# One chunk of a shared expert moved from before to behind a block loop, and a router's ranking placed ahead of a weight split

## What is computed

```
x = layernorm(x + attention(x))                        # 4096 tokens of 256
probs = softmax(x @ gate_w.T); idx = top_k(probs + gate_b, 6)
for each expert e of 16:                               # H = 176
    y += c[:, e] * ((silu(x @ W1.T + B1) * (x @ W3.T + B3)) @ W2.T + B2)
z = (silu(x @ ws1.T + bs1) * (x @ ws3.T + bs3)) @ ws2.T + bs2     # 352 wide, every token
out = layernorm(x + y + z)
```

## Time and profile before

| | |
|---|---|
| three runs, median | 1126.18 us (1124.87 to 1127.89) |
| the profiled execution | 1117.81 us, of which the span is 1115.7 |
| PE busy | 1033.5 us, 93% of the span |
| POOL, DVE, ACT busy | 738.6, 759.2, 674.3 us |
| attention, router and tiles in front | up to about 563 us |
| the loop over blocks | about 565 to 1055 us |
| behind the loop | 1055 to 1115.7 us |

### The profile page before, as it was taken

How to read it: one execution, slowest core, us unless ns; L and a number is a source line. 1 busy time by engine, 2 the same in 40 slices (tenths; PEclk the granted TensorE clock), 3 DMA queues, 4 the chain that set the end, 5 groups by cost and what they waited for, 6 DMA issues and landing times.

```text
span 1115.7 us, 28318 instructions
## 1 busy us (share of the span) xinstructions
PE 1033.5 (93%) x8028; PEld 845.6 (76%) x8029; DVE 759.2 (68%) x2406; ACT 674.3 (60%) x1680; POOL 738.6 (66%) x671
## 2 busy tenths in 40 slices
PE   7899998989999997798988999999999999999993
PEld 4546564646555553478988999999999999999993
DVE  8786878786878787668756555555555555555467
ACT  3567676767676765755545555555555555555546
POOL 4223368887888888866725666666666666666667
PEclk9999999999999999989999999999999999999997
DMA  6624254545454635466957666777776777777686
GB/s 186 184 75 115 77 141 149 166 143 159 139 172 134 180 128 163 147 214 218 293 162 165 110 117 121 117 117 118 118 120 113 119 119 117 118 117 121 114 238 237
DMA packets 127036, 163.53 MB, mean 147 GB/s; under 512 B 18800, under 2 KB 107504, under 8 KB 126704
## 3 DMA queue, kind: packets, MB, share of 16 engines
q1 hardware_dynamic: 82240, 99.73, 31.0%
q0 software_dynamic: 39024, 54.29, 27.6%
q10 hardware_dynamic: 5696, 8.55, 2.5%
HBM read 65.36 MB, written 73.85 MB: 125 GB/s over the span
## 4 chain that ended last, share of the span: by engine, by line
PE 74%; DVE 12%; ACT 4%; issue 4%; DMA 3%; POOL 2%; SPq 1%; ACTq 0%; POOLq 0%; DVEq 0%
PE psum L1061 18%; PE psum L1088 13%; PE psum L796 10%; PE psum L838 5%; PE psum L826 5%; PE psum L811 4%; PE psum L1046 4%; PE psum L1072 4%; PE psum L1057 3%; DVE rowmax L1501 3%; ACT probs L1164 2%; PE psum L1027 2%; PE psum L813 2%; PE psum L870 1%; DMA stack_q<-shift_l 1%
## 5 line engine op out<-in xcount | busy, mean ns | idle before, releaser
L1164 ACT ACTIVATE probs<-psum 128x512 f32<-128x512 f32 (+2 forms) x384 | 186.4, 529 | 115.8 <-PE psum L826 113.6
L1501 DVE TENSOR_REDUCE rowmax<-psum 128x1 f32<-128x512 f32 (+3 forms) x352 | 212.5, 633 | 60.5 <-PE psum L813 58.1
L2030 POOL DMA_INDIRECT xs_d<-x1p,index x192 | 204.5, 1065 | 52.5 <-issue 45.3
L2098 POOL DMA_INDIRECT x_d<-y_sb,tokens x104 | 162.9, 1566 | 98.6 <-ACT y_sb L1358 48.6
L2098 POOL DMA_INDIRECT z_d<-y_sb,tokens x103 | 161.2, 1565 | 81.4 <-issue 39.4
L1840 DVE TENSOR_TENSOR xb_lo<-psum,xb_hi 128x256 fp32r<-128x256 f32 x207 | 87.9, 425 | 186.2 <-ACT xb_hi L1155 186.2
L1061 PE MATMUL psum<-we_hi_lo,xb_hi 128*128 x828 | 200.6, 323 | 0.0
L1088 PE MATMUL psum<-we_hi_lo,hb_hi 88*128 (+1 forms) x828 | 174.6, 304 | 0.0
L1358 ACT ACTIVATE y_sb<-psum,combine 128x256 f32<-128x256 f32 x207 | 98.4, 475 | 125.0 <-PE psum L1088 112.4
L811 PE MATMUL psum<-stack_k,stack_q 96*128 96x256 bf16 (+3 forms) x512 | 139.0, 311 | 10.9 <-DVE rowmax L1501 4.8
L1061 PEld LDWEIGHTS psum<-we_hi_lo,xb_hi 128*128 128x128 f32 x828 | 146.6, 189 | 0.1
(11 more groups left out here) (206 smaller groups left out, 2326.4 us busy)
## 6 DMA issues: line engine op xcount, KB each, us to landing
xb<-xs_d SPq DMA_DIRECT2D x207, 138.0 KB
stack_q<-q_h SPq DMA_DIRECT2D x48, 128.0 KB
stack_k<-k_h SPq DMA_DIRECT2D x45, 128.0 KB
w_raw<-in_we SPq DMA_DIRECT2D x9, 608.0 KB, 4.4
xT_raw<-in_xT SPq DMA_DIRECT2D x9, 512.0 KB
stack_q<-q_m SPq DMA_DIRECT2D x32, 128.0 KB
stack_k<-k_m SPq DMA_DIRECT2D x32, 128.0 KB
x_res<-in_x SPq DMA_DIRECT2D x8, 512.0 KB, 3.7
```

Source lines behind the costliest of these rows:

```text
L1164: nc.scalar.activation(probs[kt][:, heads[0]:heads[0] + n, :], st[f % ST_BANKS][:, 0:n * width].rearrange("p (h t) -> p h t", h=n), ACT.Ex ...
L1501: nc.vector.reduce_max(rowmax[gpar][:, heads[0]:heads[0] + n, qt], src, AX.X).then_inc(sm_free, 1)
L2030: nc.gpsimd.indirect_dma_start(out=xs_d[:, :], out_offset=bass.IndirectOffsetOnAxis(ap=index[tp][:, n:n + 1], axis=0), in_=x1p[tp][:, n // ...
L2098: nc.gpsimd.indirect_dma_start(out=(x1_d, z_d)[k % 2][:, :], out_offset=bass.IndirectOffsetOnAxis(ap=tokens[:, k:k + 1], axis=0), in_=y_sb ...
```

## The change

1. `HC1` goes from 10 to 9: nine chunks (27 tiles) stand in front of the loop and seven (21 tiles) behind. The tile numbers of the epilogue, weights, scatters and pads stay.
2. A third turn of the block loop is written out, and three of the five late x1 chunks are loaded there (at blocks 20, 22, 23) instead of in the last turn. The other two are loaded behind the first two z loads of the finals.
3. Each late chunk is split into halves of its own (`x1T_tail`), and earlier: at T1 + 2, 3, 4, 8, 9. The hidden products behind the loop get buffers of their own.
4. The finals' statistics begin behind tile T1 + 6 instead of T1 + 8, and POOL makes 4 sums ahead instead of 3.
5. In DVE's stream, from tile 9 on, `split_w` stands behind the epilogue's stage instead of ahead of it.

```diff
-HC1 = 10
+HC1 = 9
-LATE_TURNS = 2
+LATE_TURNS = 3
-FINAL_FROM, SUMS_AHEAD = T1 + 8, 3
+FINAL_FROM, SUMS_AHEAD = T1 + 6, 4
+X1T_LATE_AT = {20: 0, 22: 1, 23: 2}
+X1T_SPLIT_AT = {2: 0, 3: 1, 4: 2, 8: 3, 9: 4}
+W_ITEM_BEHIND_STAGE = 9
...
+        def x1_halves(hc):
+
+            return X1T[hc % 2] if hc <= HC1 + 1 else X1T_tail[hc - HC1 - 2]
+
+        def hidden_of(T):
+
+            return [bufs[bank_of(T)] for bufs in (front_h if T < T1 else tail_h)]
...
         def split_x1_of(T):
 
+            if T >= T1 + 2:
+                hc = HC1 + 2 + X1T_SPLIT_AT.get(T - T1, HALVES)
+                return hc if hc < HALVES else None
...
-                    if last and k < len(x1T_late):
-                        load_x1T(HC1 + 2 + k)
+                    if isinstance(j0, int) and j0 + k in X1T_LATE_AT:
+                        sp.wait_ge(late_w_lo, 2 * LATE_W)
+                        load_x1T(HC1 + 2 + X1T_LATE_AT[j0 + k])
...
                 for i in FINAL_ORDER[:FINAL_FIRST]:
                     load_final(i, src, dst)
+                if n == 1:
+                    for hc in range(HC1 + 2 + len(X1T_LATE_AT), HALVES):
+                        load_x1T(hc)
...
-                if T in W_ITEM_AT:
+                if T in W_ITEM_AT and T < W_ITEM_BEHIND_STAGE:
                     split_w(W_ITEM_AT[T])
                 if T >= 5 and (T - 5) % ST == 0 and T < T1 - 1:
                     shared_out((T - 5) // ST)
                 epilogue(T)
+                if T in W_ITEM_AT and T >= W_ITEM_BEHIND_STAGE:
+                    split_w(W_ITEM_AT[T])
```

More of the change, by code:

```diff
@@ L244, in postln_layer @@
     phase_a = ExitStack()
-    phase_b, phase_w, phase_z, phase_l = ExitStack(), ExitStack(), ExitStack(), ExitStack()
+    phase_b, phase_w, phase_z, phase_l, phase_x = [ExitStack() for _ in range(5)]
     def sem(name):
@@ L368, in postln_layer @@
         phase_l.close()
-        hidden = [sb(f"hidden{n}", [P, HT_TOK]) for n in range(2)]
-        h_hi = [sb(f"h_hi{n}", [P, HT_TOK], f32r) for n in range(2)]
-        h_lo = [sb(f"h_lo{n}", [P, HT_TOK], f32r) for n in range(2)]
+        x1T_late = [sb(f"x1T_late{n}", [P, KD, HT_TOK], where=phase_x) for n in range(len(X1T_LATE_AT))]
+        phase_x.close()
+        front_h = [[sb(f"{name}{n}", [P, HT_TOK], dt) for n in range(2)]
+                   for name, dt in (("hidden", fp32), ("h_hi", f32r), ("h_lo", f32r))]
         X1T = [sb(f"x1T_{n}", [P, 2, KD, HT_TOK], f32r) for n in range(2)]
@@ L382, in postln_layer @@
         phase_b.close()
-        x1T_late = [sb(f"x1T_late{n}", [P, KD, HT_TOK]) for n in range(HALVES - HC1 - 2)]
+        tail_h = [[sb(f"tail_{name}{n}", [P, HT_TOK], dt) for n in range(2)]
+                  for name, dt in (("hidden", fp32), ("h_hi", f32r), ("h_lo", f32r))]
+        x1T_late += [sb(f"x1T_late{n}", [P, KD, HT_TOK]) for n in range(len(X1T_LATE_AT), HALVES - HC1 - 2)]
         fin_x = [sb(f"fin_x{n}", [P, HALF, D]) for n in range(HALVES)]
@@ L391, in postln_layer @@
         fin_shift = sb("fin_shift", [P, HALVES, HALF])
+        X1T_tail = [sb(f"x1T_tail{n}", [P, 2, KD, HT_TOK], f32r) for n in range(HALVES - HC1 - 2)]
         psum = ctx.enter_context(nc.psum_tensor("psum", [P, 8, S], fp32))
@@ L1027, in shared_down @@
                         last = nc.tensor.matmul(
-                            sum_of(hc)[:, j * D:j * D + D], (h_hi, h_lo)[a][n][:, j * P:j * P + P],
+                            sum_of(hc)[:, j * D:j * D + D], hidden_of(T)[1 + a][:, j * P:j * P + P],
                             W[b][:, t, 4:6, :].rearrange("p d n -> p (d n)"),
@@ L1253, in split_x1 @@
                 act.wait_ge(loaded, value)
-                if hc >= 2 and hc != HC1 + 1:
+                if 2 <= hc <= HC1:
                     act.wait_ge(uv_tile_full, ST * (hc - 1))
-                raw, high = in_order(src, X1T[hc % 2][:, 0], hc)
+                raw, high = in_order(src, x1_halves(hc)[:, 0], hc)
                 copy(high, raw).then_inc(x1T_hi_done, 1)
@@ L1318, in silu @@
                     act.wait_ge(h_lo_done, T - 1)
-                nc.scalar.activation(hidden[n][:], uv_ps[n][:, 0:HT_TOK], ACT.Silu,
+                nc.scalar.activation(hidden_of(T)[0][:], uv_ps[n][:, 0:HT_TOK], ACT.Silu,
                                      bias=bias[:, 0, T % ST:T % ST + 1]).then_inc(gated_done, 1)
@@ L1491, in low_x1 @@
                 dve.wait_ge(x1T_hi_done, hc + 1)
-                raw, high = in_order(src, X1T[hc % 2][:, 0].bitcast(fp32), hc)
-                low = in_order(src, X1T[hc % 2][:, 1], hc)[1]
+                raw, high = in_order(src, x1_halves(hc)[:, 0].bitcast(fp32), hc)
+                low = in_order(src, x1_halves(hc)[:, 1], hc)[1]
                 nc.vector.tensor_tensor(low, raw, high, ALU.subtract).then_inc(x1T_lo_done, 1)
@@ L1826, in low @@
                 dve.wait_ge(h_hi_done, T + 1)
[L1827 to L1829 removed]
+                raw, high, low_half = hidden_of(T)
+                nc.vector.tensor_tensor(low_half[:], raw[:], high[:].bitcast(fp32), ALU.subtract).then_inc(h_lo_done, 1)
             def shared_out(hc):
```

13 lines of the change are left out of this document (5 added, 8 removed).

## The result

The changed kernel is slower. Seven runs of it have a median of 1132.16 us (1130.15 to 1139.2), seven of the kernel before 1123.46 us; the ratio of the two sets of runs is **1.0085**, with a 95% interval of 1.006 to 1.011, that is 9.5 us (the medians by themselves are 8.7 us apart). 1124.4 was forecast, with 1129.0 as the upper end. The profiled execution takes 1136.14 us, 4.0 us above its median; its span is 1134.4, against 1117.81 and 1115.7 before. "After" is the changed kernel in what follows.

What follows compares the result with a forecast made beforehand. In front, the scatter chain, fixed by the index, was taken as the bound, with PE busy 93%. Terms -2.2 + 0.3 - 0.9 + 0.3 + 0.3 + 0.4 = -1.8 us on 1126.18 gave 1124.4 us, range 1119.6 to 1129.0.

Steps and rivals of the forecast that it cites:

- The third turn: Block loop's start: three chunk loads behind blocks 20 to 23 cost +0.3 us, between 0 and 0.9.
- extra change of turn: Block loop's start: one more written-out turn gives one more change of turn in plain code, +0.3 us, between 0 and 0.9.
- rival A: Loop's end and behind it: adds catch up fully, first sum at S + 16; total -4.9 us, 1121.3; chance 0.33.
- Behind the loop: First up behind the loop to the end: first sum at S + 19.0, PE loses 1.7 us; +0.4 us, bounds -2.3 and +3.5.
- rival B: Behind the loop: DVE at the first statistics blocks PE, +4.0 us, with the adds' lag unchanged +4.8 in all, 1131.0; chance 0.16.
- The three tiles: Behind the loop: three tiles more, 6.55 us of PE, fill the time in which POOL and DVE finish the finals.
- The ranks: In front: ranks ahead of the weight split bring the index 2.9 us earlier, the last scatter -2.2 us, bounds -2.9 and -1.0.
- The 0.7 for the split beside the first scatter: In front: the displaced weight split falls on the first scatter and slows it, taking 0.7 off the 2.9 us.
- Rival C: In front: DMA engines are the bound and scatters land when they did, no gain; sum +0.4, 1126.6 us; chance 0.1.
- Fewer tiles in front: Front: three tiles less bring nothing, PE's wait grows from 2.3 to about 7.7 us; clock restart 0.3 more, up to 1.7.
- The last turn: Block loop's end: without the late loads PE gets -0.9 us, and the last add comes 3.5 us earlier, 2.6 against PE.
- The base: Change applied to the profiled 1117.81 us, then taken as the same on the median 8.4 us above, 1126.18.

Runs made afterwards that it cites:

- b_three_turns: The kernel before with three written-out turns of the block loop in place of two, nothing else: 1127.21 us, ratio 1.0035.
- a_loads_last: The changed kernel with its three late chunk loads moved from the third turn to the last turn (blocks 200 to 202): 1125.62 us, ratio 1.003.
- a_two_final8: The changed kernel with two written-out turns, its three loads in the last turn, first statistics behind T1 + 8 and three sums ahead: 1123.72 us, ratio 1.0006.
- a_final8: The changed kernel with the first statistics behind tile T1 + 8 and three sums ahead, as before the change: ratio 1.0063.
- b_nine: The kernel before with only HC1 = 9, five late chunks being loaded in the last turn: 1126.92 us, ratio 1.0049.
- b_ranks_2: The kernel before with only the ranks' epilogue ahead of the weight split on DVE, run again on another chip: 1119.9 us, ratio 0.9972.
- b_y6_2: The kernel before with three written-out turns, eight weighted-row buffers and a wait for the add of six blocks ago, on another chip: 1117.17 us, ratio 0.9955.
- b_again: The kernel before, unchanged, profiled once more, on the chip where everything lay near 1153 us: ratio 1.0028.
- b_ranks: The kernel before with only the ranks' epilogue ahead of the weight split, on the chip where everything lay near 1153 us: ratio 1.0007.

## Why the prediction was wrong, step by step

**The third turn: the step that failed.** The prediction put the loads there at +0.3 us, "between 0 and the 0.9 that four cost", since "the adds have just been given slack by the late weights", and the extra change of turn at +0.3. From block 24 to 200 the profiled pair lost 13.9 us instead, and without the third turn, its loads and the statistics' place the loss in the runs is gone (1.0006). What it measured by was the rows' loads: they do keep ahead. What it left out is that the slack is 1 to 3 us under a limit of 5.4, that the loads take some of it (lag at block 18: 4.9 to 6.7), and that hardly anything gives it back, because the adds' spacing of 4.56 is "just the two blocks' 4.58". That sentence stood in rival A, as a reason why a lag is kept, and was not carried to the place where a lag is made with 180 blocks still to come. The four loads of the last turn cost 0.9 because the loop ended 7 blocks later. The mechanism: what delays the adds is paid once at the end of the loop; at its start, once the lag is at its limit, it is paid in every turn, some 0.4 us each. The limit's part is shown by the room for six blocks (420.2 against 408.7 us). The extra change of turn, +0.3, belongs to the same step: by itself it was 1.0035, about 4 us, in b_three_turns, and nothing can be told from 0 in the changed kernel (a_loads_last 1.003, a_two_final8 1.0006 with the statistics' 0.0022 in it). The loads in the changed kernel were worth about 6 us (1.0085 to 1.003); in the kernel before, where 1.0063 and 1.0035 overlap, their share is not told. What tips the loop in a given execution is not settled beyond that, as a_loads_last and a_final8 show.

**Behind the loop: rival B.** The forecast of +0.4 became +6.7 in the profiled pair; B had this part at 4.0 more, and 2.6 more again "with the adds' lag unchanged", +7.0 in all, and its mechanism is what came: DVE blocks PE at the first statistics. The delay came from elsewhere than B had it, more from the adds than from the loads. The last add did not start 2.6 us earlier against S, but at S + 11.6, since the adds were at the limit, whatever the last turn had in it. From its start to that of the first sum 9.5 us passed instead of 8.3: the chunk loads in SP's queue cost about 1.2 us, not 0.5 (in all traces it is 8.6 to 10.0 us with them and 6.7 to 8.3 without). So the first sum ended at S + 22.4 instead of 19.0, the low half came so much later, and PE lost 5.6 instead of 1.7 us, with 1.4 more for the clock, which the sum did not have. B's threshold, a first sum at S + 24.2, is not reached. That B's 1131.0 lies near the measured 1132.16 is luck: most of the profiled difference arose in the loop, where B had no more than the forecast's +0.6. The three tiles are the second mis-sized term: b_nine and a_final8 lose 4.0 and 3.4 us without a blocked DVE, where the prediction let them vanish in the time of the finals.

**The ranks: right, and too low.** From the router's matmul to the index it was 14.25 us; in b_ranks_2 it is 10.96 (516.39 to 527.35), 3.3 us less; after has the same 10.96. 2.9 was worked out. The 0.7 for the split beside the first scatter was wrong, because the scatter starts 1.03 us behind the index and only 0.48 us of the split is left by then: it took 1.31 us in b_ranks_2, and 1.35 in b_y6_2, where no split stands there. Scatters that lie longer beside a split do pay: in b_ranks_2 one with 1.28 us beside it took 2.11 us and one with 1.07 took 1.90, against 0.96 to 1.03 alone. For these the trace agrees with the rule on the shared port pair that the prediction took from the Trainium skill, "SBUF — State Buffer"; the 0.48 us beside the first scatter cost nothing that shows. The gain by the ratio is 3.1 us. Rival C falls, if narrowly: the interval ends at 0.9993. In the profiled execution of after the gain doesn't meet the eye, since the router's matmul was 3.6 us later (514.27): attention varies by that much.

**Fewer tiles in front: right as far as it went.** PE waited 8.60 us for the first rows (7 to 8 forecast); the clock behind it:

```profile
563.00:569.00 6.00, 4.42 (x20) 4.42 (x21) 1.62 (x9) 1.14 (x3) 0.39 (x2) 0.50 0.44 119
```

0.50 against 0.72 in the earlier trace rows. In that window PE still stood until 564.58. Counted over the 6 us from its first rows on, the granted clock is 0.55 after (from 564.58) and 0.74 before (from 565.50), which loses 2.7 us against 1.6: 1.1 more, within the bounds given, not 0.3.

**The last turn**, -0.9: -0.3, for the reason above.

**The base.** One trace was taken as the kernel's time, 8.4 us below the median of the three runs. "The change is the same" was a guess: b_again, the same program, has 5.6 us more from block 24 to 200, so some of those 8.4 us are the other state of the loop. Rival A's sum has a slip: its terms, with the forecast's others, give -4.4 and not -4.9 us, which changes no chance.

## What to carry to other kernels

- When two chains that wait for each other have nearly the same period, ask at each place what gives a delay back before the next comes. A delay that is never given back costs nothing until it meets a limit (buffers here), and then it costs in every round. Here the same transfers were cheap in the last turn and cost about 6 us in the third.
- Look at the lag between producer and consumer, and at the limit that the buffers set to it, not only at waits: before, the waits for adds were 5 us in all in the loop, and the lag stood 1 to 2 us under its limit.
- One profiled execution can be in a state that the median isn't in. Profile the unchanged kernel twice before differences of a percent are explained; and room on the consumer's side (six blocks instead of four) was worth 0.8% where the moved work was worth less than nothing.

## What was not expected of the hardware

- Adds with indices, 128 rows of 1 KB each: POOL needs 1.56 us to issue one, and it lands 3.8 us (before) to 4.0 us (after) behind its issue. Evenly spaced at 2.3 us two into one tensor are 4.5 to 4.6 apart, in pairs of 1.9 and 2.8 they are 4.7. Why pairs land later is open.
- The adds of blocks 60, 113 and 119 come late by 0.8 to 1.5 us in before, b_again and b_three_turns alike (gaps of 3.1 to 3.8 us between adds that are 2.3 apart otherwise; b_again lacks the first). The instruction queues are silent there. The four loops that tip late (b_again, b_ranks, b_nine, a_two_final8) do so between blocks 115 and 125, around the last two. The cause is open.
- The kernel before had a median of 1122 to 1124 us in four sets of runs and of 1153 us in one, on another chip; there, in b_again, block 0 came at 604 instead of 569 us.
